# K'V of a window attention in 64-row array tiles: v spread into four window places, a plain and a pooled visit per tile, transposes a tile later

## The reference

```
x = x + conv3x3(groupnorm(x))
x = x + batchnorm(proj(attention(qkv(groupnorm(x)))))
```

```
kv  = relu(k)^T [v, 1]          (8 x 9, per window and head)
out = relu(q) kv                (16 x 9)
out = out[:, :8] / (out[:, 8:] + 1e-15)
```

## Time and profile before

| | |
|---|---|
| median of 3 runs | 2616.96 us (2615.79 to 2617.56) |
| the profiled execution's own time | 2621.07 us |
| its span | 2619.1 us |
| mean granted TensorE clock | 0.985 |
| TensorE busy | 2520.5 us, 96% |
| VectorE busy | 1660.5 us, 63% |
| ScalarE busy | 1202.7 us, 46% |
| GpSimd busy | 776.7 us, 30% |

### The profile page before, as it was taken

How to read it: one execution, slowest core, us unless ns; L and a number is a source line. 1 busy time by engine, 2 the same in 40 slices (tenths; PEclk the granted TensorE clock), 3 DMA queues, 4 the chain that set the end, 5 groups by cost and what they waited for, 6 DMA issues and landing times.

```text
span 2619.1 us, 136962 instructions
## 1 busy us (share of the span) xinstructions
PE 2520.5 (96%) x62112; PEld 2272.2 (87%) x62112; DVE 1660.5 (63%) x3403; ACT 1202.7 (46%) x3152; POOL 776.7 (30%) x2164
## 2 busy tenths in 40 slices
PE   5999999999999999999999999999999999999998
PEld 5988889888898888988889888897889978898887
DVE  7875558655586555865558655685556855564564
ACT  2136651366414664146631566325662256622665
POOL 0014430244302442034420344103441034411443
PEclk9999999999999999999999999999999999998999
DMA  4000010000100001000010000100001000000000
GB/s 158 1 2 15 18 57 11 2 18 14 66 3 6 14 18 64 1 6 18 14 65 1 9 14 18 61 1 9 18 18 58 1 9 18 18 9 2 15 18 19
DMA packets 38943, 57.97 MB, mean 22 GB/s; under 512 B 4688, under 2 KB 36304, under 8 KB 36560
## 3 DMA queue, kind: packets, MB, share of 16 engines
q1 hardware_dynamic: 38736, 55.27, 6.0%
HBM read 29.57 MB, written 25.69 MB: 21 GB/s over the span
## 4 chain that ended last, share of the span: by engine, by line
PE 96%; issue 2%; DVE 1%; ACT 1%; DMA 0%; POOL 0%; SPq 0%; POOLq 0%; DVEq 0%
PE ps L317 31%; PE ps L389 15%; PE ps L363 12%; PE ps L336 11%; PE ps L378 9%; PE ps L343 8%; PE ps L352 4%; PE ps L399 3%; PE ps L302 0%; DMA xs<-w_conv 0%; PE ps L507 0%; DVE st L715 0%; ACT ve L567 0%; ACT yb L594 0%; PE ps L328 0%
## 5 line engine op out<-in xcount | busy, mean ns | idle before, releaser
L317 PE MATMUL ps<-dp,wc 128*128 128x392 f32 x4608 | 834.0, 341 | 1.1 <-issue 1.1
L317 PEld LDWEIGHTS ps<-dp,wc 128*128 128x128 f32 x4608 | 816.4, 188 | 2.3 <-issue 1.4
L892 DVE TENSOR_TENSOR kvm<-ps,hm 128x1152 f32<-128x1152 f32 (+1 forms) x200 | 266.6, 1333 | 375.0 <-PE ps L363 375.0
L389 PE MATMUL ps<-at,wp 128*128 128x128 f32 (+1 forms) x3200 | 416.1, 284 | 9.0 <-ACT at L602 5.4
L1070 POOL TENSOR_TENSOR xs<-yb,xs 128x128 f32<-128x128 f32 (+3 forms) x560 | 197.7, 381 | 719.2 <-ACT yb L594 719.2
L389 PEld LDWEIGHTS ps<-at,wp 128*128 128x128 f32 x3200 | 379.2, 194 | 19.3 <-ACT at L602 7.1
L539 ACT CAST dp<-dt 128x896 fp32r<-128x896 f32 x128 | 120.9, 945 | 563.1 <-PE ps L317 473.7
L1041 POOL TENSOR_TENSOR qm<-qraw 128x64 f32<-128x64 f32 x200 | 59.5, 297 | 1042.0 <-ACT qraw L578 1042.0
L363 PE MATMUL ps<-ve,kr 32*32 32x72 f32 x25088 | 346.5, 234 | 17.9 <-issue 6.9
L363 PEld LDWEIGHTS ps<-ve,kr 32*32 32x32 f32 x25088 | 272.8, 104 | 90.0 <-issue 78.8
L336 PE MATMUL ps<-wkv,xt 128*128 128x512 f32 x1200 | 333.6, 414 | 0.0
(11 more groups left out here) (87 smaller groups left out, 2948.1 us busy)
## 6 DMA issues: line engine op xcount, KB each, us to landing
out<-xs SPq DMA_DIRECT2D x224, 112.0 KB, 1.8
xs<-x SPq DMA_DIRECT2D x16, 1344.0 KB, 8.8
xs<-x SPq DMA_DIRECT2D x16, 224.0 KB, 2.7
xs<-w_conv SPq DMA_DIRECT2D x1, 2304.0 KB, 8.8
kvm<-w_kv SPq DMA_DIRECT2D x1, 512.0 KB, 14.4
wp<-w_proj SPq DMA_DIRECT2D x4, 128.0 KB, 8.0
wq<-w_q SPq DMA_DIRECT2D x1, 256.0 KB, 14.1
gav<-gavg SPq DMA_DIRECT2D x1, 64.0 KB, 8.5
```

The source lines that it names most:

```text
L317: last = nc.tensor.matmul(ps[:, BANK_C[kk % 2][mt], 0:CONV_N], wc[:, part_w, k, kt * TAPS + dy, mt * P:(mt + 1) * P], dp[:, kk % 2, part_d ...
L389: last = nc.tensor.matmul(ps[:, BANK_Q, mt * TT:mt * TT + n], wp[:, q, mt * P:(mt + 1) * P], at[:, q, e, 0:n], start=(q == 0), stop=(q == ...
L892: nc.vector.tensor_tensor(kvm[:, :, 0:n].rearrange("p h r c -> p r h c"), ps[:, BANK_A:BANK_A + n, 0:8 * QW].rearrange("p r (h c) -> p r h ...
```

## The change

- K'V products take 64 rows, four windows, at a time: `kr[64 * r:64 * r + 64]` against v in four places (PLACES), 144 columns. There are 16 products for a set instead of 32, on 8 array tiles of 64 rows and 32 columns, and each row group writes a bank of its own (plain: BANK_A, BANK_A + 1; pooled: BANK_A + 2, + 3).
- The two sets are two visits with other work between them. The order on TensorE in a tile becomes: K'V plain, q of s+1, transposes of s-1, k and v of s+1, K'V pooled, projection of s-1, attention of s, pooling of s+1.
- ScalarE writes v of the plain set into four places by four ACTIVATEs; of the pooled set it writes one plain copy, `vpraw`. GpSimd spreads that into four places by one multiplication with `vmask` (`spread_pooled`), after `add_tile`. TensorE's `keys_values` waits for `vp_raw`, its pooled visit for `vp_ready`.
- VectorE masks each set by itself (576 elements in a partition, twice), and does `weights` and `outputs` last in a tile.
- ScalarE's copies of the transposes (`turned`) come right after q.

In the final tile the transposes of tile 23 come between its two visits; in tile 0 there are neither transposes nor a projection.

```diff
@@ keys_times_values (TensorE)
                 for gg in range(2):
-                    for r in range(2 * units):
+                    for r in range(units):
                         for q in range(QUADS):
...
-                                ps[32 * q:32 * q + 32, BANK_A + r, (h * 2 + gg) * 2 * QW:(h * 2 + gg + 1) * 2 * QW],
-                                kr[32 * r:32 * r + 32, e, k0:k0 + 32],
-                                ve[32 * r:32 * r + 32, e, :, h, v0:v0 + QW], start=True, stop=True)
-                if h == 1:
-                    last.then_inc(ktv_done, 1)
+                                ps[32 * q:32 * q + 32, BANK_A + 2 * h + r, gg * PLACES * QW:(gg + 1) * PLACES * QW],
+                                kr[64 * r:64 * r + 64, e, k0:k0 + 32],
+                                ve[64 * r:64 * r + 64, e, :, h, v0:v0 + QW], start=True, stop=True)
+                last.then_inc(ktv_done, 1)
@@ tile (TensorE), as it stands after
+                pe.wait_ge(v_ready, n1)
+                keys_times_values(0, e, units)
+                if not first:
+                    if not final:
+                        pe.wait_ge(xh_low, n2)
+                        pe.wait_ge(y_ready, n0)
+                        q_of_tile(1 - e)
+                    pe.wait_ge(ao_ready, n0)
+                    turn(2)
+                if not final:
+                    pe.wait_ge(vp_raw, n1)
+                    keys_values(n2, 1 - e)
...
+                pe.wait_ge(vp_ready, n1)
+                keys_times_values(1, e, units)
+                if not first:
+                    pe.wait_ge(at_ready, n0)
...
+                    project(1 - e, 2)
...
+                pe.wait_ge(masked, masks)
...
+                attend(e, units)
+                if not final:
+                    pooled(n2)
@@ keys_values, pooled_keys_values (ScalarE)
-                for e in range(2):
+                for e in range(PLACES):
...
-                for e in range(2):
-                    last = nc.scalar.activation(
-                        ve[:, t % 2, e, 1].rearrange("p (n m) -> p n m", m=DIM + 1)[:, :, 0:DIM],
-                        ps[0:TT, BANK_KV, C:2 * C].rearrange("p (n m) -> p n m", m=DIM),
-                        ACT.Copy, scale=vmaskp[:, e:e + 1])
-                last.then_inc(vp_ready, 1)
+                if b or t:
+                    act.wait_ge(vp_ready, b * TILES + t)
+                nc.scalar.activation(vpraw[:], ps[0:TT, BANK_KV, C:2 * C], ACT.Copy, scale=POOL_SCALE).then_inc(vp_raw, 1)
@@ attention (VectorE)
-                    mask(b, s)
+                    mask(b, s, 0)
                     if s + 2 < TILES:
                         normalize_tile(b, s + 2)
-                    weights(b, s)
+                    mask(b, s, 1)
                     if s + 1 < TILES:
                         kv_low_part(b, s + 1)
-                    outputs(b, s)
                     if s + 2 < TILES:
                         tile_low(b, s + 2)
                     if s + 1 < TILES:
                         pooled_q(b, s + 1)
+                    weights(b, s)
+                    outputs(b, s)
@@ GpSimd
+            def spread_pooled(b, t):
+                pool.wait_ge(vp_raw, b * TILES + t + 1)
...
+                nc.gpsimd.tensor_tensor(
+                    ve[:, t % 2, :, 1].rearrange("p e (n m) -> p e n m", m=DIM + 1)[:, :, :, 0:DIM],
+                    vpraw[:].rearrange("p (n m) -> p n m", m=DIM).unsqueeze(1).to_broadcast([TT, PLACES, C // DIM, DIM]),
+                    vmask[:].unsqueeze(2).unsqueeze(3).to_broadcast([TT, PLACES, C // DIM, DIM]),
+                    ALU.mult).then_inc(vp_ready, 1)
```

More of the change, by code:

```diff
@@ L53 @@
 HEADS_Q = 32 // DIM
+PLACES = 4
 QW = HEADS_Q * (DIM + 1)
@@ L416, in tile @@
                 keys_times_values(1, e, units)
[L418 to L421, removed]
-                        pe.wait_ge(y_ready, n0)
-                        q_of_tile(1 - e)
-                    keys_values(n2, 1 - e)
-                else:
-                    pe.wait_ge(at_ready, n0)
-                    pe.wait_ge(y_ready, n0)
+                if not first:
+                    pe.wait_ge(at_ready, n0)
+                    if not final:
+                        pe.wait_ge(q_ready, n2)
+                    else:
+                        pe.wait_ge(y_ready, n0)
                     project(1 - e, 2)
                 pe.wait_ge(w_loaded, DMA)
-                pe.wait_ge(masked, n1)
+                pe.wait_ge(masked, masks)
                 pe.wait_ge(q_ready, n1)
                 pe.wait_ge(qp_ready, n1)
-                if not first:
-                    pe.wait_ge(at_ready, n0)
                 attend(e, units)
                 if not final:
-                    if not first:
-                        pe.wait_ge(at_ready, n0)
-                        pe.wait_ge(q_ready, n2)
-                        project(1 - e, 2)
                     pooled(n2)
-                    turn(n1, units)
             def attention(b):
@@ L525, in _ @@
                 attention(b)
[L526 removed]
+            pe.wait_ge(ao_ready, B * TILES)
+            turn(1)
             last_tile(B - 1)
@@ L610, in attention @@
                         q_of_tile(b, s + 1)
+                    if s >= 1:
+                        turned(b, s - 1)
+                    if s + 1 < TILES:
                         keys_values(b, s + 1)
@@ L886, in outputs, with mask @@
                     ALU.mult).then_inc(ao_ready, 1)
[L888 to L891 removed]
+            def mask(b, t, h):
+                n = tile_units(t)
+                dve.wait_ge(ktv_done, 2 * (b * TILES + t) + h + 1)
                 nc.vector.tensor_tensor(
[L893 to L895 removed]
+                    kvm[:, h, 0:n].rearrange("p r (g c) -> p r g c", g=2),
+                    ps[:, BANK_A + 2 * h:BANK_A + 2 * h + n, 0:2 * PLACES * QW].rearrange("p r (g c) -> p r g c", g=2),
+                    hm4[:].unsqueeze(1).unsqueeze(1).to_broadcast([P, n, 2, PLACES * QW]),
                     ALU.mult).then_inc(masked, 1)
@@ L994, in _ @@
             dve.wait_ge(set_up, 2)
-            for n in range(4):
+            for n in range(PLACES):
                 last = nc.vector.tensor_copy(hm4[:, n * QW:(n + 1) * QW].rearrange("p (i m) -> p i m", m=DIM + 1),
@@ L998, in _ @@
             last.then_inc(set_up, 1)
-            for e in range(2):
-                last = nc.vector.tensor_reduce(vmask[:, e:e + 1], vwin[:, e::2], AXIS.X, ALU.add)
+            for e in range(PLACES):
+                last = nc.vector.tensor_reduce(vmask[:, e:e + 1], vwin[:, e::PLACES], AXIS.X, ALU.add)
             last.then_inc(set_up, 1)
             dve.wait_ge(set_up, 4)
-            nc.vector.tensor_scalar(vmaskp[:], vmask[:], POOL_SCALE, None, ALU.mult).then_inc(set_up, 1)
             for par in range(2):
-                for e in range(2):
+                for e in range(PLACES):
                     last = nc.vector.tensor_copy(
@@ L1063, in pool_q @@
                                         ALU.add).then_inc(qsum_ready, 1)
+            def spread_pooled(b, t):
+                pool.wait_ge(vp_raw, b * TILES + t + 1)
+                if b == 0 and t == 0:
+                    pool.wait_ge(set_up, SET_UP)
+                nc.gpsimd.tensor_tensor(
[3 more added lines that the diff above has]
+                    ALU.mult).then_inc(vp_ready, 1)
             def add_tile(b, t):
```

46 lines of the change are left out of this document (20 added, 26 removed).

## The result

| | before | changed |
|---|---|---|
| median of the runs | 2616.85 us (2615.79 to 2617.56, 4 runs) | 2534.88 us (2533.41 to 2536.54, 4 runs) |
| ratio | | 0.9687, 95% interval 0.967 to 0.9704 |
| profiled execution | 2621.07 us | 2534.49 us |
| its span | 2619.1 us | 2532.7 us |
| mean granted TensorE clock | 0.985 | 0.995 |

The account below looks back on a forecast made before the run. TensorE, busy for 96% of the span, was taken as the bound. Per image, loop tiles -5.8, tile 0 -1.1 and tile 24 +1.9 us gave -5.0, times 8 -40: a median of 2577 us, range 2538 to 2650.

Parts of the forecast that it names:

- The visit, v: One K'V visit on TensorE: 0.64 us instead of 0.87, from 0.51 of streams plus 0.13 to the next group.
- bound by streams: Rival for K'V visits: 1.12 us each with a fixed rest of 0.61, total 2769; with a milder variant, chance 0.10.
- Two more changes of form: TensorE switching between small array tiles and full array, one island more per tile: 0.20 us added, bounds 0 and 0.27.
- The tile of the loop: Regular attention tile on TensorE: 8.08 us instead of 8.33, over 23 tiles -5.8 us per image.
- The spread: GpSimd's multiplication of pooled v into four places: 2.4 us, between 2.3 and 3.1, hidden in the loop by 0.12.
- Tile 0 and tile 24: An image's irregular tiles: tile 0 saves 1.1 us; tile 24 loses 1.9, as nothing covers the spread.
- The sum: All tiles together: -5.0 us per image, -40 over eight images, median 2577 us.
- the clock: TensorE idling more in tile 24: one more low-clock stretch per image costs 22 us, 2599; in the range, no chance given.
- A sign: What would show it, on TensorE: K'V's records falling from 25088 to about 6270.
- The rivals: Other outcomes: GpSimd late 0.14, visit bound by streams 0.10, VectorE's end of tile late 0.16, best case 0.08.
- the third: Rival on VectorE: normalize held up by the spread delays the transposes, tile 8.2 to 8.3, 2600 to 2618 us; chance 0.16.
- GpSimd rival: Late GpSimd: spread of 3.1 us, or 2.4 and a hold-up, loop tile 8.66, total 2690 us; chance 0.14.

Follow-up runs that it names:

- e7: Changed kernel with K'V products of 72 columns, places 0 and 1 alone, same number of instructions, half of K'V left out: 2461.42 us.
- e1: Changed kernel with K'V again in array tiles of 32 rows, products of 72 columns, everything else in the new order: 2640.82 us.
- e2: Kernel before with K'V in array tiles of 64 rows, v's four places written by ScalarE for both sets, old order: 2743.46 us.
- e4: Changed kernel with GpSimd's spread done a second time into a spare tensor in every tile: 2781.32 us (one run).
- e3: Changed kernel with ScalarE writing the pooled v into the four places in an image's final tile, no GpSimd spread there: 2519.79 us.

## Why the prediction was wrong

- **The visit, v.** 0.64 predicted, 0.65 measured; e7 shows that it is the streams, and the final tile of before was the right row to double. The bound by streams of the rivals, with its fixed rest of 0.61, is excluded: the fixed rest is 0.65 - 0.48 = 0.17.
- **Two more changes of form.** 0.20 predicted; 8.09 - 8.33 + 1.73 - 1.30 = 0.19.
- **The tile of the loop.** 8.08 predicted, 8.09 measured, no wait in it.
- **The spread.** 2.4 us taken between 2.3 and 3.1; it is 1.9, below my lower end. The line of the profile:

```profile
L1071 POOL TENSOR_TENSOR ve<-vpraw,vmask x200: 1893/1895/1899, 165.5 to 2518.4; 128x1024 f32<-128x1024 f32 x100
```

  (1895 - 252) / 992 = 1.66 ns an element, against the 2.1 that I drew from instructions of 32 and 128 elements. The slope between these short instructions overstated the long one. It left more slack, and made tile 24 shorter than worked out.
- **Tile 0 and tile 24.** -1.1 predicted for tile 0; the shortest ones are 6.10 against 7.15, -1.05. For tile 24 it was 6.7 against 4.75, +1.9; without the low clock it is 6.18, +1.4, since the spread is 0.5 us shorter than taken. The mean one is 7.23 against 4.63, +2.6: the low clock came on top.
- **The sum.** This is the step that failed. It added up TensorE's work and its semaphore waits, and left the kernel's 2% of "issue" and its low clock as they were, with the clock as a possible loss only ("One more such stretch per image would cost 22 us"). Tiles 1 and 23 were counted as regular tiles, though tile 23 took 11.5 us on average and tile 1 10.6, and the wait of 1.45 us in tile 0 was priced at its length, without the low clock behind it. What the sum did count came to 42 us against its 40. What it left out is the 42 us that it lacks: stalls fell from 32.8 to 8.1 us, which goes with the form of K'V (e1, e2), and the loss to the low clock from 38 to 12 us, most of it in tiles 0 to 3, where it took form and order together. How the 42 us divide between the two is not shown, since they overlap. The new wait in tile 24 did bring the low clock there in five of the first seven images, as feared, and was outweighed.
- **A sign.** K'V's records were to fall to "about 6270". They fell from 25088 to 12544, which is what 16 products instead of 32 give; the 6270 halved twice, and nothing in the sum rests on it. The wait of pooling for `kv_part` fell from 11.7 us to 1.7, and the wait for `ve` in tile 24 is 1.19 us instead of 1.5.
- **The rivals.** None of them happened. GpSimd was not late; by e4 the spread begins to set the tile at 2.6 us, where the prediction's loop has 2.4 + 0.12 = 2.5. VectorE's `normalize_tile` was held up, as the third had it, but not enough to delay the transposes: see the last section.

The profile of before had it: tiles 1 to 23 at 8.33 make 191.6 us, and with tiles 0 and 24 some 203.5, while the stage takes 211. The 7.4 us in between had no place in my sum, so I could not see that the change would touch them.

## What to carry to other kernels

Lay a stage out tile by tile before costing a change: what the regular tile does not explain is a term of its own, and "issue" waits and the clock behind them belong in the sum. An "issue" wait is a stall only if no semaphore's work ended just before its end; the packets of the instruction queue beside it tell. Fewer, larger instructions pay a second time where code is new; with small instructions a loop, whose code is not brought again (104 packets against 393), is worth more than straight-line code. A new wait costs its length and the slow work behind it: e3 took 0.8 us of wait out of a tile and got 1.8.

## What the runs showed of the hardware that was not expected

- TensorE's instruction supply can be short for products of some 19 ns each (the attention's 64 in 1.22 us): the stalls end 1.0 to 1.7 us after a packet of instructions, and straight-line code of the same work cost 104 us with 456 records a tile and 218 us with 584.
- VectorE and GpSimd: the spread is never held up (1893 to 1899 ns over 200), VectorE is. `normalize_tile` beside it, from the changed kernel's and the old kernel's lines:

```profile
L853 DVE TENSOR_SCALAR xh<-xs,gn x560: 289/345/1315, 152.4 to 2504.1; 128x128 f32<-128x128 f32 x74, 128x96 f32<-128x96 f32 x38, 128x64 f32<-128x64 f32 x38, 128x32 f32<-128x32 f32 x37
```
```profile
L852 DVE TENSOR_SCALAR xh<-xs,gn x560: 290/340/395, 152.1 to 2589.7; 128x128 f32<-128x128 f32 x74, 128x96 f32<-128x96 f32 x38, 128x64 f32<-128x64 f32 x38, 128x32 f32<-128x32 f32 x37
```

  In the tile above the first of two starts at 1256.05 and ends at 1257.28, just behind the spread (1255.30 to 1257.19); the second takes 344 ns. Each of the 175 records of that line over 600 ns ends within 0.25 us of the end of a spread. The GpSimd rival had the hold-up on GpSimd's side, from its row of 1057 ns; both sides occur (that line is at 1052 at worst in the changed kernel).
- On array tiles of 64 rows and 32 columns eight float32 streams ran side by side at the rate of one: 0.83 ns a column and record in e7, against 0.88 taken from the full array.
